# A wait of TensorE on its own gate-and-up count in every routed pair of an AdaLN block with a mixture of experts

## The reference

```python
probs = jax.nn.softmax(xt @ w_router, axis=-1)
top_w, top_i = jax.lax.top_k(probs, TOP_K)
top_w = top_w / jnp.sum(top_w, axis=-1, keepdims=True)
...
g = jax.nn.silu(jnp.einsum('td,edh->teh', xt, we1)) * jnp.einsum('td,edh->teh', xt, we3)
g = g * cw[:, :, None]
moe_out = jnp.einsum('teh,ehd->td', g, we2)
shared = jax.nn.silu(xt @ ws1) * (xt @ ws3) @ ws2
out = shared / (k + 1) + moe_out * (k / (k + 1))
```

## Time and profile before

| what | value |
|---|---|
| median of three runs | 340.33 us (340.19 to 340.52) |
| span of the profiled execution, first to last instruction | 380.7 us |
| time of the profiled execution beside its span | none given |
| mean granted TensorE clock | 0.990 |
| PE, PEld busy | 88%, 78% of the span |
| DVE, POOL, ACT busy | 67%, 53%, 50% |

### The profile page before, as it was taken

One profiled execution on the slowest core, in us unless ns is written; L12 is line 12 of the kernel. 1 busy time (PEld: TensorE's weight loads), 2 busy tenths in 40 slices (PEclk: granted clock), 3 DMA queues, 4 the chain that ended last, 5 costly groups with the idle time before them and its releaser, 6 DMA issues.

```text
span 380.7 us, 7758 instructions
## 1 busy us (share of the span) xinstructions
PE 333.3 (88%) x2252; PEld 297.6 (78%) x2252; DVE 255.2 (67%) x806; ACT 190.3 (50%) x440; POOL 200.8 (53%) x285
## 2 busy tenths in 40 slices
PE   8989999999999999868889897788778877887995
PEld 5778898888899898736778796777667767877784
DVE  1889998999887756219986744543454345448797
ACT  2667777767865665414234444443444355346300
POOL 2687754357867655746740064555455545545820
PEclk9999999999999999969999999999999999999999
DMA  8236600002213996322232466556445544788824
GB/s 271 75 104 205 209 17 27 16 31 87 85 65 118 316 312 214 119 85 78 104 117 76 121 209 183 155 171 194 149 124 171 164 133 136 264 302 327 261 86 165
DMA packets 42280, 57.55 MB, mean 151 GB/s; under 512 B 5144, under 2 KB 34592, under 8 KB 42240
## 3 DMA queue, kind: packets, MB, share of 16 engines
q1 hardware_dynamic: 34288, 35.42, 30.7%
q0 software_dynamic: 6864, 19.80, 13.5%
q10 hardware_dynamic: 1088, 1.84, 1.5%
HBM read 32.64 MB, written 24.40 MB: 150 GB/s over the span
## 4 chain that ended last, share of the span: by engine, by line
PE 43%; DVE 27%; issue 13%; another core or an unknown queue 7%; ACT 7%; DMA 1%; POOL 1%; DVEq 0%; ACTq 0%
PE ps L1816 10%; PE ps L1818 10%; PE ps L1817 9%; PE ps L1990 4%; DVE y_in L1497 3%; DVE r_g L1771 2%; DVE gT_lo L1759 2%; ACT r_silu L1083 2%; DVE negmax L1626 2%; PE ps L2191 2%; PE ps L2092 1%; PE ps L1823 1%; DMA wmod_sb<-in_L_wmod_dram 1%; DVE bn L1197 1%
## 5 line engine op out<-in xcount | busy, mean ns | idle before, releaser
L817 POOL DMA_INDIRECT y_rows<-y_sb,aside x72 | 70.5, 980 | 87.9 <-ACT y_sb L1092 71.7
L776 POOL DMA_INDIRECT xg_rows<-hrow,slot_u x64 | 65.6, 1024 | 27.8 <-issue 20.0
L1816 PE MATMUL ps<-rpool 128*128 128x256 f32 (+3 forms) x152 | 49.8, 328 | 2.7 <-DVE rpool L1221 1.1
L1768 DVE TENSOR_TENSOR aside<-ends,aside 128x2 int32<-128x2 int32 (+1 forms) x40 | 6.3, 157 | 62.9 <-ACT r_silu L1083 55.4
L1816 PE MATMUL ps<-w_hi_routed,xT_hi 128*128 x158 | 45.2, 286 | 1.8 <-DVE xT_lo L1752 1.8
L1083 ACT ACTIVATE r_silu<-ps 128x256 f32<-128x256 f32 x40 | 15.8, 395 | 61.4 <-PE ps L1818 51.4
L1818 PE MATMUL ps<-rpool 128*128 128x256 f32 (+3 forms) x152 | 46.0, 302 | 0.0
L1817 PE MATMUL ps<-rpool 128*128 128x256 f32 (+3 forms) x152 | 45.9, 302 | 0.0
L1818 PE MATMUL ps<-w_hi_routed,xT_lo 128*128 x158 | 44.7, 283 | 0.0
L1817 PE MATMUL ps<-w_lo_routed,xT_hi 128*128 x158 | 44.6, 283 | 0.0
L1816 PE MATMUL ps<-w_hi_routed,gT_hi 128*128 x79 | 25.8, 326 | 15.1 <-DVE gT_lo L1759 15.0
(11 more groups left out here) (236 smaller groups left out, 928.8 us busy)
## 6 DMA issues: line engine op xcount, KB each, us to landing
xs<-xg_rows SPq DMA_DIRECT2D x68, 144.0 KB
y_in<-y_rows SPq DMA_DIRECT2D x16, 512.0 KB
xg_rows<-empty SPq DMA_DIRECT2D x4, 576.0 KB, 3.8
x_in<-in_L_attn_x_dram SPq DMA_DIRECT2D x16, 128.0 KB, 2.1
w_raw_routed<-in_L_ffn_we_dram SPq DMA_DIRECT2D x8, 256.0 KB
out_dram<-x SPq DMA_DIRECT2D x14, 128.0 KB, 1.8
xs_own<-xg_rows SPq DMA_DIRECT2D x11, 144.0 KB
wmod_sb<-in_L_wmod_dram ACTq DMA_DIRECT2D x3, 512.0 KB, 6.6
```

Of the source, the lines that this page charges most:

```text
L776: nc.gpsimd.indirect_dma_start(out=xg, out_offset=bass.IndirectOffsetOnAxis(ap=slot_u[:, t, k:k + 1].bitcast(U32), axis=0), in_=hrow[:, t, ...
L817: nc.gpsimd.indirect_dma_start(out=yb, out_offset=bass.IndirectOffsetOnAxis(ap=dest[:, 2 * n + i:2 * n + i + 1].bitcast(U32), axis=0), in_ ...
L1816: nc.tensor.matmul(dst, w[0], x_[0], start=first, stop=False)
```

## The change

One wait is added to TensorE's list. In every iteration n below 40, behind the transposes of `rows_back(n + 2)` and ahead of those of `g_back(n - 1)`, TensorE waits until `s_rgu` has reached n + 1, that is until its own last product of `rows_gate_up(n)` has been announced. In iteration 0, which has no `g_back`, the wait falls on the register step ahead of the next pair's products.

```diff
--- before.py
+++ after.py
@@ -2245,6 +2245,8 @@
                     rows_gate_up(n, of[n])
                 if n + 2 < NPAIR:
                     rows_back(n + 2)
+                if n < NPAIR:
+                    pe.wait_ge(s_rgu, n + 1)
                 if 0 <= n - 1 < NPAIR:
                     g_back(n - 1)
                 if n == NPAIR + 1:
```

## The result

Twenty runs of the changed kernel have a median of **341.85 us** (339.76 to 343.19), twenty of the kernel before 340.19 us (338.74 to 340.63). The ratio is 1.0051, with a 95% interval of 1.0038 to 1.0064: the change costs 1.7 us, with an interval of 1.3 to 2.2 us. The profiled execution of the changed kernel took 342.11 us, with a span of 340.4 us.

The account below looks back on a forecast made before the run. PE was taken to bound the routed pairs at 2.81 us each; usual pairs 0, two loads 1.4 and last two iterations 0.1 made +1.5 us on the median of 340.33, so 341.8 us, range 339.6 to 345.4.

Parts of the forecast that it names:

- Do the runs have late announcements?: PE's product announced 2.85 us late in every second routed pair of the trace; the timed runs should have next to none.
- the 40.4 us: Excess of the first trace's span, 380.7 us, over the runs' median of 340.33; late announcements in it were sized at 42.1 us.
- The rule of the Trainium skill: Updates fire when their instruction completes, so no announcement would be late; the first trace's 2.85 us contradicted it.
- The usual pair: 36 pairs, timed from s, the last gate-and-up product's start: `rows_back` covers wait and `rows_down` register step; 0 us.
- The two loads: Expert-number loads queued on PE's sequencer behind the `rows_down` register step start 0.71 us later, uncovered: 1.4 us for both.
- The last two iterations: Iterations 38 and 39, without `rows_back`: PE delayed 0.28 us in each, mostly hidden by waiting for DVE; 0.1 us.
- every pair pays: Rival: in the usual pairs the wait's release costs one step more, 0.10 us times 36; 345.4 us, chance 0.10.
- the loads are covered everywhere: Rival: the loads' 0.71 us vanish behind POOL or a later low part of g; 340.3 to 340.9 us, chance 0.27.
- the runs have the late announcements: Rival: timed runs have them too, and the wait ahead of line 2217 removes them; 316 to 328 us, chance 0.13.

Follow-up runs that it names:

- second profiled execution: The kernel before, unchanged, profiled once more: 339.31 us, span 337.6 us.
- two experiments that split the waits: The changed kernel's wait in all iterations but 9 and 17 (340.18 us, ratio 1.0003), and in 9 and 17 alone (342.12 us, ratio 1.0067).
- the best version: The kernel before without added wait, expert-number loads halved and moved behind the gate-and-up register steps, DVE's column-number loads moved ahead of the g product: 339.04 us, ratio 0.9965.
- the 38 waits that cost nothing: The changed kernel with the wait left out in iterations 9 and 17, ahead of the loads of expert numbers: 340.18 us, ratio 1.0003.

## Why the prediction was right

The forecast was 341.8 us, +1.5; measured were 341.85 us, +1.7. That the two times agree to 0.05 us is luck: the cost came out 0.2 us larger, and the kernel before 0.14 us faster (340.19 in place of 340.33). Its steps, one by one:

- **Do the runs have late announcements?** No, as it concluded from the 40.4 us: undisturbed, the kernel before has a span of 337.6 us and pairs of 2.81 us, and 71 of its 72 runs in the three comparisons took 338.07 to 340.94 us, where a span of 380.7 would make some 382 (an estimate, with the 1.7 us by which the second profiled execution's time exceeds its span). What it said behind that was off: it took the late announcements to come with the profiled execution as such, and let the new wait bring the profiled span down by 10 to 25 us. The span fell by 40.3 us, and the wait had no part in that which these runs can show, since the unchanged kernel's fell too, and so did those of four more kernels that lack the wait in most pairs or in all. PE never stood before line 2217 in an iteration of the changed kernel that has its four transposes. What the wait would do in an execution with late announcements was not seen.
- **The rule of the Trainium skill** (PSUM — Partial Sum Buffer, Engine vs sequencer instructions), by which an update fires when its instruction completes, fits the changed kernel and all eight others, where the silu follows 0.04 us behind in all 40 pairs. The first profiled execution, with its 2.85 us, remains the one measurement against it.
- **The usual pair, nothing.** Right: line 2217 at s + 0.56, `rows_down` at s + 0.69, 2.81 us. The step went at s + 0.45 where s + 0.43 was forecast. Putting the wait ahead of the transposes showed that they are the cover, worth 0.27 us a pair.
- **The two loads, 1.4 us.** Right in mechanism and nearly in size. Forecast: load at s + 0.93, product at s + 2.49, 1.00 us bare, 0.29 bare before. Measured: load at s + 0.93, product at s + 2.43, and pairs of 3.84 and 3.92 us, 1.03 and 1.11 over 2.81; undisturbed before 3.13 and 3.05, so 0.32 and 0.24. The difference is 1.6 us. The 0.2 us beyond the forecast are mostly the second load, which lasted 1334 ns in the one trace and 1107 ns in the other. The forecast took 1.3 us for every load; the last section shows that loads behind the wait took 0.2 us more on average than those without one, which the forecast did not have. The two experiments that split the waits showed that this term is all of the cost that the runs can tell.
- **The last two iterations, 0.1 us.** The delay on PE was as forecast, 0.30 us in iteration 38, and it is covered, as the trace's tail shows; the runs with that wait alone, at +0.1 us with an interval of -0.5 to +0.8, agree but could not tell it alone. Iteration 37 was counted as a usual pair, wrongly: pair 39 has one tile, so two transposes stand ahead of the wait in place of four, and the pair took 2.68 us in place of 2.59. That is 0.09 us, below what a run can tell.
- **What it left out:** the four register loads of DVE. They cost much the same before and after, about 0.1 us for each of the four pairs (0.57 us in all after, 0.37 before), so the difference did not need them; the best version did.
- **The rivals.** That every pair pays fell with the 38 waits that cost nothing. That the loads are covered everywhere fell for this order of instructions, and holds where the loads stand ahead of the wait. That the runs have the late announcements fell with the second trace of before.

## What to carry to other kernels

A wait that is free for the instructions right behind it may still not be free for the slow one at the end of the queue: here 46 ns steps could be 0.7 us late without harm, and a register load of 1.2 us could not. So, wherever a wait is added, look down the same sequencer's list for the next long instruction and ask how much of the lead it was using; better, put such a load where the sequencer is ahead of its engine. When a profiled execution is much longer than the median of the runs, first put the missing time in places, and then size a change on the pairs that run undisturbed.

## What was not expected of the hardware

The same kernel was profiled twice with spans of 380.7 and 337.6 us. In the longer one the announcement of a PE product came 2.85 us late in every second pair of a long stretch, and once DVE waited 11.37 us for one; none of the nine later profiled executions (of before, the changed kernel and seven variants) shows one. The semaphore records of that first trace show that the announcements themselves were held, and not ACT. In the iteration of the earlier trace rows the products and transposes that raise `s_rgu`, `s_rxT`, `s_rgT` and `s_rdown` ended at 241.28, 241.72, 241.94 and 242.65 us; the four counts rose at 244.11, 244.19, 244.23 and 244.31, within 0.2 us of each other, while PE went on with the next pair. The cause stays open: nothing here brought it back.

A register load of 16 expert numbers took 1107 to 1542 ns in the routed pairs, one of 8 numbers 587 to 963 ns, and its length changes from one execution to the next for the same instruction. It also goes with the place: the six loads of 16 behind an added wait (the changed kernel and two variants) took 1237 to 1542 ns, mean 1.37 us, the six in the undisturbed kernels without a wait there 1107 to 1249, mean 1.13 us. Why is not shown. The Trainium skill (Runtime: NRT & Kernel Launch, Instruction fetch mechanics) states some 200 ns per register for such a load. The traces do not agree: these loads, from a tile on the chip, show 69 to 120 ns for each number.

In the profile the added wait itself has no row. It does leave a mark beside it: the wait for `s_rg`, which the transpose of line 2217 carried before, becomes an instruction of the sequencer, with these rows in the changed kernel and none in the kernel before. They run ahead of the new wait, and the usual pair's 2.81 us show no cost of them.

```profile
L2213 PEldq EVENT_SEMAPHORE  x37: 51/51/51, 208.1 to 311.2; - x37
```

The Trainium skill (Perfetto Trace Analysis, Sequencer-only Instruction) says that the reported time of a sequencer's instruction begins once its semaphores are satisfied, and the traces agree: the register step behind the wait, 0.7 us later than before, still reads 46 ns. The length of such a wait is read from the start times of what stands behind it, and from no duration.
